# Threshold search by a clamp between two prepared candidates, instead of a compare and an XOR

## What is computed

```python
probs = jax.nn.softmax(logits, axis=-1)
_, idx = jax.lax.top_k(logits.T, top_k)          # top_k = capacity = 8192 / 16 = 512
xe = xn[idx]
h = jax.nn.gelu(jnp.einsum('ecd,efd->ecf', xe, fc1_weight) + fc1_bias[:, None, :], approximate=False)
y = jnp.einsum('ecf,edf->ecd', h, fc2_weight) + fc2_bias[:, None, :]
```

## Time and profile before

| | |
|---|---|
| Median of 3 runs | 980.95 us |
| The profiled execution | 983.5 us, its span 981.8 us |
| Granted TensorE clock, mean | 0.929 of full |
| TensorE matmul busy | 861.1 us (88%) |
| VectorE busy | 747.0 us (76%) |
| ScalarE busy | 505.8 us (52%) |
| GpSimd busy | 591.7 us (60%) |

### The profile page before, as it was taken

One profiled execution on the slowest core, in us unless ns is written; L12 is line 12 of the kernel. 1 busy time (PEld: TensorE's weight loads), 2 busy tenths in 40 slices (PEclk: granted clock), 3 DMA queues, 4 the chain that ended last, 5 costly groups with the idle time before them and its releaser, 6 DMA issues. The chain is left out here.

```text
span 981.8 us, 20963 instructions
## 1 busy us (share of the span) xinstructions
PE 861.1 (88%) x6115; PEld 737.1 (75%) x6115; DVE 747.0 (76%) x1660; ACT 505.8 (52%) x921; POOL 591.7 (60%) x564
## 2 busy tenths in 40 slices
PE   7899999999999999998711149999999999999995
PEld 6678887888788887886510037989999999999985
DVE  4488888888888888887388965898777777777642
ACT  1356556655566556655256206465555555555531
POOL 4256667666676667665442264688876776775344
PEclk8799999999999999999755559999999999999998
DMA  5266666666566656654232033366766555665333
GB/s 161 92 202 226 207 207 206 213 219 208 192 212 222 207 204 205 212 193 157 75 103 83 3 88 127 113 196 181 183 162 157 159 155 161 161 175 153 85 70 43
DMA packets 129540, 156.51 MB, mean 159 GB/s; under 512 B 22464, under 2 KB 104656, under 8 KB 129376
## 3 DMA queue, kind: packets, MB, share of 16 engines
q1 hardware_dynamic: 104096, 113.06, 35.5%
q0 software_dynamic: 15616, 25.70, 12.1%
q10 hardware_dynamic: 9792, 17.31, 4.8%
HBM read 74.93 MB, written 26.28 MB: 103 GB/s over the span
## 5 line engine op out<-in xcount | busy, mean ns | idle before, releaser
L587 DVE TENSOR_REDUCE NM<-bank 128x4 f32<-128x480 f32 x256 | 155.4, 649 | 59.9 <-PE bank L745 59.9
L418 ACT ACTIVATE PT<-bank 120x512 f32<-120x512 f32 x256 | 142.8, 603 | 35.9 <-PE bank L770 34.7
L349 POOL TENSOR_SCALAR XN<-X,mv,rstd 128x256 f32<-128x256 f32 x124 | 150.5, 1222 | 14.1 <-POOL rstd L344 13.3
L1658 PE MATMUL bank<-W2H,HH 128*128 128x256 f32 x512 | 145.5, 284 | 2.0 <-issue 2.0
L1660 PE MATMUL bank<-W2H,HL 128*128 128x256 f32 x512 | 144.3, 282 | 0.0
L1659 PE MATMUL bank<-W2L,HH 128*128 128x256 f32 x512 | 144.3, 282 | 0.0
L1119 POOL DMA_INDIRECT out_dram<-C,IO x60 | 109.6, 1827 | 52.2 <-issue 31.3
L1387 DVE TENSOR_TENSOR HL<-hf,HH 128x512 fp32r<-128x512 f32 x128 | 87.5, 691 | 49.8 <-ACT HH L1542 49.3
L545 DVE RECIPROCAL RR<-RC 128x256 f32<-128x256 f32 x64 | 111.6, 1743 | 8.6 <-DMA RC<-PVS 8.6
L770 PE MATMUL bank<-QX,KX 128*120 128x256 f32 x512 | 110.8, 309 | 8.2 <-DMA QX<-NMT 5.0
L1537 ACT ACTIVATE hf<-bank,B 128x512 f32<-128x512 f32 x128 | 87.8, 686 | 40.9 <-PE bank L1660 35.6
(11 more groups left out here) (194 smaller groups left out, 1906.6 us busy)
## 6 DMA issues: line engine op xcount, KB each, us to landing
QX<-QH ACTq DMA_DIRECT2D x64, 256.0 KB
W<-w1T_dram SPq DMA_DIRECT2D x16, 1024.0 KB, 5.3
W<-w2T_dram SPq DMA_DIRECT2D x16, 1024.0 KB, 5.9
X<-x_dram SPq DMA_DIRECT2D x32, 256.0 KB, 3.0
QX<-QL SPq DMA_DIRECT2D x32, 256.0 KB
XB<-x_dram SPq DMA_DIRECT2D x32, 256.0 KB, 2.8
RC<-PVS SPq DMA_DIRECT2D x64, 128.0 KB, 2.1
OC<-PVS SPq DMA_DIRECT2D x64, 128.0 KB, 2.2
```

Of the source, the lines that this page charges most:

```text
L349: ins = pool.tensor_scalar(dst[:, t, :], src[:, t, :], mv[:, t, 0:1], rstd[:, t:t + 1], ALU.subtract, ALU.mult)
L418: act.activation(PT[u][0:M, HE * k:HE * (k + 1), :], score_bank(b, k // 2)[k % 2][0:M, :], ACT.Exp, scale=SCALE) \
L587: dve.tensor_reduce(NM[u][:, t, :].rearrange("p (f n e) -> p n e f", n=HN, e=HE)[:, n, :, :], smax_bank[q % 2][:, 0:4 * M].rearrange("p (e ...
L1658: pe.matmul(o, wh, xh, start=first, stop=False)
```

## The change

The total is now the signed distance to the limit, scaled by 2^113, so it is either below every candidate or above every candidate. The two candidates that can follow are prepared while the total is on its way, and one operation clamps the total between them: `min(max(total, nexts[0]), nexts[1])` gives `nexts[0]` for a negative total and `nexts[1]` for a positive one.

- The limit comes in by a third matmul, `same_big` times a column of the new tile `limits`, which stands first in each round's group and ahead of the wait for the count. The weights `same_big` are `same_e` times 2^113 in bf16; the columns stay fp16.
- The group's bank alternates between two (`sum_bank`).
- `nexts` is one XOR of the candidate with two masks, one column each (`steps`): the next bit, and the tried bit with the next bit. It stands ahead of the shift, which now moves both masks, and the wait between them falls away.
- `missed` and the XOR behind it become the one clamp, with the total as its tensor and the two columns of `nexts` as pointers. A round has two increments of `step_dve` instead of three.
- GpSimd's constants: the cast becomes a multiplication with 2^113, and a memset, a wait, four memsets and a wait are added.

```diff
-def search_constants(pool, consts, same_e, same_e_below, same_e16, zero_row):
+def search_constants(pool, consts, same_e, same_e_below, same_big, zero_row, limits):
...
-    pool.tensor_copy(same_e16[:, :], same_e[:, :]).then_inc(consts, 1)
+    pool.tensor_scalar(same_big[:, :], same_e[:, :], BIG, 0.0, ALU.mult, ALU.add).then_inc(consts, 1)
+    pool.memset(limits[:, :], 0.0).then_inc(consts, 1)
+    pool.wait_ge(consts, n + 3)
+    for v, limit in enumerate((GMAX, SMAX)):
+        whole = -math.copysign(math.floor(abs(limit)), limit)
+        pool.memset(limits[0:E, v:v + 1], whole).then_inc(consts, 1)
+        pool.memset(limits[2 * E:3 * E, v:v + 1], -limit - whole).then_inc(consts, 1)
+    pool.wait_ge(consts, n + 7)
...
-    minus_half_e = sb("minus_half_e", [P, P], FP16)
+    minus_half_e = sb("minus_half_e", [P, P], BF16)
...
+    sum_bank = bank[2:4]
...
-            m = 3 * ROUNDS * turn + (BASE + 3 * r)
+            m = 2 * ROUNDS * turn + (BASE + 2 * r)
...
-            dve.tensor_scalar(bit[(r + 1) % 2][:, :], bit[r % 2][:, :], 1, None, ALU.logical_shift_right) \
+            dve.wait_ge(bit_ready, ROUNDS * turn + (r + 2))
+            dve.tensor_scalar(nexts[:, :], steps[r % 2][:, :], cand[:, :], None, ALU.bitwise_xor).then_inc(step_dve, 1)
+            dve.tensor_scalar(steps[(r + 1) % 2][:, :], steps[r % 2][:, :], 1, None, ALU.logical_shift_right) \
                 .then_inc(bit_ready, 1)
-            dve.wait_ge(bit_ready, ROUNDS * turn + (r + 2))
-            dve.tensor_scalar(both[:, :], cand[:, :], bit[(r + 1) % 2][:, :], None, ALU.bitwise_xor).then_inc(step_dve, 1)
+            dve.wait_ge(step_dve, m + 1)
             dve.wait_ge(total_done, ROUNDS * turn + (r + 2))
-            dve.tensor_scalar(missed[:, :], cnt_bank[:, 0:1], GMAX if alone else SMAX, bit[r % 2][:, :], ALU.is_lt, ALU.mult) \
-                .then_inc(step_dve, 1)
+            dve.tensor_scalar(cand[:, :].bitcast(FP32), sum_bank[(r + 1) % 2][:, 0:1], nexts[:, 0:1].bitcast(FP32),
+                              nexts[:, 1:2].bitcast(FP32), ALU.max, ALU.min).then_inc(step_dve, 1)
             dve.wait_ge(step_dve, m + 2)
-            dve.tensor_scalar(cand[:, :], both[:, :], missed[:, :], None, ALU.bitwise_xor).then_inc(step_dve, 1)
-            dve.wait_ge(step_dve, m + 3)
...
-        dve.memset(bit[0][:, :], 1 << 30).then_inc(bit_ready, 1)
+        dve.memset(top_bit[:, :], 1 << 30).then_inc(bit_ready, 1)
+        dve.memset(steps[0][:, 0:1], 3 << 29)
+        dve.memset(steps[0][:, 1:2], 1 << 29).then_inc(bit_ready, 1)
...
+            own = sum_bank[r % 2][:, 0:1]
+            v = 0 if alone else 1
+            pe.matmul(own, same_big[:, :], limits[:, v:v + 1], start=True, stop=False)
             pe.wait_ge(count_ready, ROUNDS * turn + (r + 1))
-            ins = pe.matmul(cnt_bank[:, 0:1], same_e16[:, :], count16[:, :], start=True, stop=alone)
+            ins = pe.matmul(own, same_big[:, :], count16[:, :], start=False, stop=alone)
             if not alone:
                 pe.wait_ge(signs_ready, ROUNDS * turn + (r - ALONE))
-                ins = pe.matmul(cnt_bank[:, 0:1], minus_half_e[:, :], sign16[:, :], start=False, stop=True)
+                ins = pe.matmul(own, minus_half_e[:, :], sign16[:, :], start=False, stop=True)
             ins.then_inc(total_done, 1)
```

More of the change, by code:

```diff
@@ L3 @@
 from contextlib import ExitStack
+import math
 FP32 = mybir.dt.float32
@@ L47 @@
 SMAX = GMAX - NC * HT / 2
+BIG = 2.0 ** 113
 BASE = 3
@@ L937, in routed_phase @@
     LT, LP, odd, sign_of, _ = search_views(search_tiles)
-    same_e, same_e_below, same_e16, zero_row = search_consts
+    same_e, same_e_below, same_big, zero_row, limits = search_consts
     probs = sb("probs", [P, NT, E], FP32)
@@ L970, in routed_phase @@
     ranked2 = sb("ranked2", [P, 2, CT], FP32)
-    cand, missed, both = (sb(n, [P, 1], U32) for n in ("cand", "missed", "both"))
-    bit = [sb(f"bit{u}", [P, 1], U32) for u in range(2)]
+    cand, top_bit = sb("cand", [P, 1], U32), sb("top_bit", [P, 1], U32)
+    steps = [sb(f"steps{u}", [P, 2], U32) for u in range(2)]
+    nexts = sb("nexts", [P, 2], U32)
     missed_i, cand_i = (sb(n, [P, 1], I32) for n in ("missed_i", "cand_i"))
@@ L1121, in add_up @@
                     .then_inc(added, 16)
-        pool.tensor_scalar(minus_half_e[:, :], same_e16[:, :], -0.5, 0.0, ALU.mult, ALU.add).then_inc(weights_ready, 1)
+        pool.tensor_scalar(minus_half_e[:, :], same_big[:, :], -0.5, 0.0, ALU.mult, ALU.add).then_inc(weights_ready, 1)
         pool.iota(s_col[:, :], pattern=[[1, GT]], base=0, channel_multiplier=GT,
@@ L1216, in decide @@
                               accum_out=count16[:, :]).then_inc(count_ready, 1)
-            dve.tensor_scalar(bit[(r + 1) % 2][:, :], bit[r % 2][:, :], 1, None, ALU.logical_shift_right) \
+            dve.wait_ge(bit_ready, ROUNDS * turn + (r + 2))
+            dve.tensor_scalar(nexts[:, :], steps[r % 2][:, :], cand[:, :], None, ALU.bitwise_xor).then_inc(step_dve, 1)
+            dve.tensor_scalar(steps[(r + 1) % 2][:, :], steps[r % 2][:, :], 1, None, ALU.logical_shift_right) \
                 .then_inc(bit_ready, 1)
-            dve.wait_ge(bit_ready, ROUNDS * turn + (r + 2))
-            dve.tensor_scalar(both[:, :], cand[:, :], bit[(r + 1) % 2][:, :], None, ALU.bitwise_xor).then_inc(step_dve, 1)
+            dve.wait_ge(step_dve, m + 1)
             dve.wait_ge(total_done, ROUNDS * turn + (r + 2))
-            dve.tensor_scalar(missed[:, :], cnt_bank[:, 0:1], GMAX if alone else SMAX, bit[r % 2][:, :], ALU.is_lt, ALU.mult) \
-                .then_inc(step_dve, 1)
+            dve.tensor_scalar(cand[:, :].bitcast(FP32), sum_bank[(r + 1) % 2][:, 0:1], nexts[:, 0:1].bitcast(FP32),
+                              nexts[:, 1:2].bitcast(FP32), ALU.max, ALU.min).then_inc(step_dve, 1)
             dve.wait_ge(step_dve, m + 2)
-            dve.tensor_scalar(cand[:, :], both[:, :], missed[:, :], None, ALU.bitwise_xor).then_inc(step_dve, 1)
-            dve.wait_ge(step_dve, m + 3)
         dve.tensor_scalar(junk, LT, 0.0, None, ALU.is_ge, ALU.add, accum_out=count16[:, :]).then_inc(count_ready, 1)
-        dve.memset(bit[0][:, :], 1 << 30).then_inc(bit_ready, 1)
+        dve.memset(top_bit[:, :], 1 << 30).then_inc(bit_ready, 1)
+        dve.memset(steps[0][:, 0:1], 3 << 29)
+        dve.memset(steps[0][:, 1:2], 1 << 29).then_inc(bit_ready, 1)
         dve.wait_ge(total_done, 1)
-        then(dve.tensor_scalar(missed_i[:, :], cnt_bank[:, 0:1], GMAX, None, ALU.is_lt))
+        then(dve.tensor_scalar(missed_i[:, :], sum_bank[0][:, 0:1], 0.0, None, ALU.is_lt))
         then(dve.tensor_scalar(cand_i[:, :], missed_i[:, :], 31, 31, ALU.logical_shift_left, ALU.arith_shift_right))
         dve.wait_ge(bit_ready, 1)
-        then(dve.tensor_scalar(cand[:, :], cand_i[:, :].bitcast(U32), bit[0][:, :], None, ALU.bitwise_xor))
+        then(dve.tensor_scalar(cand[:, :], cand_i[:, :].bitcast(U32), top_bit[:, :], None, ALU.bitwise_xor))
         assert n[0] == BASE
@@ L1241, in _ @@
         decide(0, 30, True)
-        n[0] = BASE + 3 * 31
+        n[0] = BASE + 2 * 31
         dve.wait_ge(sum_ready, 4)
@@ L1557, in signs @@
         def signs(r):
-            act.wait_ge(step_dve, BASE + 3 * r)
+            act.wait_ge(step_dve, BASE + 2 * r)
             with nc.allow_low_precision(reason="a whole number of at most 512"):
@@ L1768, in program @@
         search_consts = [ctx.enter_context(nc.sbuf_tensor(name, shape, dt)) for name, shape, dt in
-                         (("same_e", [P, P], FP32), ("same_e_below", [P, P], FP32), ("same_e16", [P, P], FP16),
-                          ("zero_row", [P, CT], FP32))]
+                         (("same_e", [P, P], FP32), ("same_e_below", [P, P], FP32), ("same_big", [P, P], BF16),
+                          ("zero_row", [P, CT], FP32), ("limits", [P, 2], FP16))]
         search_tiles = [ctx.enter_context(nc.sbuf_tensor(name, shape, FP32)) for name, shape in
```

## The result

The changed kernel takes 986.0 us (median of 22 runs) against 983.71 for the kernel before on the same chip (22 runs): ratio 1.0037, 95% interval 1.0024 to 1.005. I had forecast 975.3 and a gain of 5.7 us; by the ratio it is 3.6 us slower (2.3 by the two medians), inside the half per cent that I called "same", outside my range and on the other side of no change.

A forecast was written before the change was run, and what follows sets the result against it. The prediction took VectorE's serial chain to bound the search and TensorE the expert loop. The clamp's -6.2 us and GpSimd's constants' +0.5 summed to -5.7, taking the median 980.95 to 975.3; range 972.5 to 979.8.

The forecast's parts named there:

- The round's path: Search rounds: one clamp replaces `missed` and the XOR, saving 0.20 us a round, 6.2 us over 31 rounds.
- a free pointer: Rival for the clamp: its second pointer costs nothing, saving 8.0 us less 0.5, giving 973.5; chance 0.15.
- a merged operation as dear as what it replaces: Rival for the clamp: only 0.06 us a round saved, gain 1.9 us less 0.5, giving 979.6; chance 0.08.
- The start of the clamp: Search rounds: the clamp starts 0.03 us behind the last matmul's end, in a round of 1.40 us.
- The masks: Search rounds: `nexts` and the shift finish by the time the total arrives, at no cost.
- the step doesn't leave the path: Search rival: `nexts` and the shift release the clamp 0.15 us late, losing 4.7 of 6.2 us, giving 980.0; chance 0.08.
- GpSimd's constants: Tail of attention: the added memsets and waits delay `ve` and are paid in full, 0.5 us, bounds 0.2 and 1.0.
- ScalarE: Search rounds with a weight copy: no cost, 0.07 us idle left; as rival bound 976.5, chance 0.10.
- the extra matmul: Search rounds: the limit's matmul, 0.19 us, fits in TensorE's 1.35 us idle time and costs nothing.
- the mixed types: Rival for the search's matmuls: bf16 with fp16 adds 0.39 us each, 23 us in all, giving 998; chance 0.04.
- The clock: Rival behind the search: full clock returns later, 10 us more products at the lower level cost 5, giving 980.3; chance 0.05.

The follow-up runs named there:

- e4_wait_before_shift: Changed kernel with the wait for `nexts` moved from between shift and clamp to between `nexts` and shift; ratio 1.004 to the kernel before.
- e1_single_columns: Changed kernel with `nexts` and the mask shift each made one column at a time, four operations instead of two; ratio 0.998 to the kernel before.
- e5_masks_in_psum: Changed kernel with the two-column masks `steps` in PSUM and the wait for `nexts` ahead of the shift; 976.66 us, ratio 0.9924 to the kernel before.
- e8_constants_three_times: Kernel before with the change's memsets and waits for the limits added three times over; ratio 1.0026 to the kernel before.
- e2: Kernel before with its mask tile `bit` two columns wide, all readers taking the first column; ratio 1.0064 to the kernel before.
- e7: Changed kernel with masks and `nexts` three columns wide instead of two, the third unused; ratio 1.0042 to the kernel before.
- e6_limits_at_start: As e5_masks_in_psum, with the memsets of `limits` and their waits moved to the kernel's start; 975.89 us, ratio 0.9928 to the kernel before.

## Why the prediction was wrong

**The round's path: right in mechanism, and the size of the clamp too.** The clamp was to take 0.278 and takes 0.276 to 0.280. So the second pointer costs the 0.06 read from the earlier trace rows, no run shows one that comes for nothing, and the rivals of a free pointer and of a merged operation as dear as what it replaces fall. With the latter falls the 61 ns, an estimate from the table in the Trainium skill ("VectorE: DVE Perf Modes", section "The TRN2 errata"), for the operation that went.

```profile
L1234 DVE TENSOR_SCALAR cand<-bank,nexts x31: 276/278/280, 497.2 to 552.7; 128x1 f32<-128x1 f32 x31
```

**The start of the clamp: a mis-sized term.** I let it start 0.03 behind the matmul, as `missed` does. It starts 0.10 behind (516.09, 516.19), because the change also leaves two waits in a row ahead of it (e4_wait_before_shift). I had counted the wait for `nexts` as free since `nexts` is early. The round is 1.48, not 1.40, and the saving 3.8 us (e1_single_columns against before), not 6.2. Moved, it is 5.7 (e5_masks_in_psum).

**The masks: the step that failed.** I wrote "I cost them at nothing", and named as their cover the accumulator read and the matmuls. The cost isn't in the operation's place or length but in what it shares. e1_single_columns and the changed kernel differ by it alone: 50.85 against 59.59, so 8.7 us. The rival "the step doesn't leave the path" came nearest, with a wrong cause and half the size: in the five rounds the clamp is indeed released by the masks. I had looked only at what VectorE's queue holds, not at what runs on GpSimd in those rounds, where before the change this subtraction starts in the round of the earlier trace rows:

```profile
517.29 4.52 POOL L1138 TENSOR_TENSOR W2L<-W,W2H 128x2048 fp32r<-128x2048 f32 x1 [3.67 <-ACT W2H L1578]
```

And the trace of before most likely has the effect already, in a line next to one that I used as the price of two pointers:

```profile
L524 DVE TENSOR_SCALAR XN<-X,mv,rstd x2: 395/1545/2695, 6.7 to 9.3; 128x256 f32<-128x256 f32 x2
```

```profile
5.84 1.79 POOL L362 MEMSET QX<- 128x2048 f32 x1
6.73 3.01 DVE L524 TENSOR_SCALAR XN<-X,mv,rstd 128x256 f32<-128x256 f32 x2
7.58 1.69 POOL L363 MEMSET KX<- 128x1920 f32 x1
```

It is the same operation in the same shape as that of the earlier trace rows, at 2.695 us instead of 0.408. It starts during the first of two GpSimd memsets that write SBUF one behind the other, and it ends at 9.43, 0.16 behind the second. A line whose longest instruction is seven times its shortest should have been asked for its neighbours.

The Trainium skill names the mechanism. Its page "SBUF — State Buffer", section "Who interferes with whom", says that VectorE and GpSimd share a pair of ports, that whichever issues first keeps it for its whole instruction, and that copy, cast and tensor_scalar can take it while the form that also writes its accumulator can't. The Trainium skill, "VectorE: DVE Perf Modes", section "Mode 2×_2P", gives the condition: source and destination in SBUF, and an outermost dimension, not counting those of length one, that is even, or odd and equal on both sides. The runs agree with what they can show of both pages, which are the times and not the ports: held at two and at three columns (3.78), not at one (0.210), not from PSUM (0.216), and the counts, which write an accumulator, keep their 0.745 beside the same GpSimd work. By this rule, and with the 4.5 us of a subtraction in the trace of before, the change's forecast would have been a saving less four or five blocks of up to 4.5 us, and the likeliest case would have been slower. One thing in the trace of before isn't explained by the order of issue: `XN` had been waiting since 6.73 and was still held by the memset that began at 7.58.

**GpSimd's constants: right in mechanism, too small.** 0.5 was forecast, `ve` starts 1.16 behind the last table's start instead of 0.38, so 0.8. The term that was too small is the start of one memset behind the other: those of `limits` start 0.15 apart and not 0.04.

```profile
463.82 0.30 POOL L909 TENSOR_SCALAR same_big<-same_e 128x128 bf16<-128x128 f32 x1
464.07 0.09 POOL L910 MEMSET limits<- 128x2 f16 x1
464.22 0.09 POOL L914 MEMSET limits<- 16x1 f16 x1
464.37 0.09 POOL L915 MEMSET limits<- 16x1 f16 x1
...
464.98 0.19 POOL L344 TENSOR_SCALAR ve<-mv 128x2 f32<-128x2 f32 x1 [0.22 <-POOL limits L915]
```

Why 0.15 isn't shown. It isn't the 16 partitions alone: at the start of the kernel before, `no_max` is set on 16 partitions too and starts 0.03 behind the memset ahead of it (1.52, 1.55). That it is paid in full holds (e8_constants_three_times).

**ScalarE, the extra matmul, the mixed types: right.** ScalarE starts within 0.01 us of VectorE in the rounds of 1.41 with a copy too (e4_wait_before_shift, 516.00). The limit's matmul runs behind the total, 0.17 long, and the count's keeps 0.19 at the most. The price of the rival with the mixed types was misread, though: the earlier trace rows has two matmuls in its 0.58, and one takes 0.36, so the rival stood for 10 us and not 23.

```profile
L1644 PE MATMUL bank<-counts,same_e x2: 353/362/372, 552.4 to 552.7; 128*128 128x2 f32 x2
```

The count's and the limit's in the changed kernel:

```profile
L1645 PE MATMUL bank<-count,same_big x32: 183/187/187, 494.7 to 552.4; 128*128 128x1 f16 x32
L1643 PE MATMUL bank<-limits,same_big x32: 163/165/186, 493.7 to 550.5; 128*128 128x1 f16 x32
```

**The clock: a rival of the right kind with the gain, not the loss.** The rest of the span differs, as far as I can follow it, by the clock and, before the search, by the 0.8 us of constants. The granted clock is 0.91 up to 20 us and 0.87 from there to 60 in the changed kernel, against 0.83 in both stretches before, and the last table's operation starts 0.92 earlier (463.82, 464.74). The first fence is of before, the second of the changed kernel: stretch, then busy us of PE, PEld, DVE, ACT and POOL, then the granted clock.

```profile
480.00:486.00 6.00, 4.96 (x20) 4.02 (x20) 1.44 (x3) 0.33 (x1) 1.84 (x2) 0.72 0.12 44
602.70:607.20 4.50, 4.50 (x13) 3.54 (x14) 2.03 (x5) 0.69 (x1) 2.17 (x3) 0.62 0.27 87
```

```profile
480.00:486.00 6.00, 4.15 (x28) 3.70 (x28) 1.77 (x6) 0.84 (x2) 2.97 (x4) 1.00 0.25 87
606.40:611.00 4.60, 4.60 (x20) 3.83 (x21) 2.32 (x6) 2.08 (x4) 2.31 (x2) 1.00 0.28 86
```

The second expert's first products begin at 602.69 and at 606.40. Before, the clock falls back to its lower level within them (0.62 on average), after the change it doesn't (1.00). It is the same in the projection of the tail at 480.67 and 480.92, 3.68 us long before and 1.99 after; in the 6 us from 470 on it is the other way round, 0.72 before and 0.50 after. In the profiles, what follows the reciprocal takes 432.3 us before the change, 432.1 in e1_single_columns and e5_masks_in_psum, 430.5 after the change, and 429.1 to 429.3 in e2, e7 and e8. So the five whose search ended later than that of before (552.97 to 558.09 us) got 1.7 to 3.3 us back in these profiles, which goes with the ratios of the slow kernels being milder than their searches. It isn't a rule: e6_limits_at_start, which ends its search earliest (543.87), has 430.3, and the gain of e5_masks_in_psum is above its own search too (7.5 us, 4.9 to 9.9, where search less constants give 4.9). Nor is what comes before the search steady from one profile to the next: the first count starts between 493.3 and 495.0 in eight of the ten, but at 499.48 in e5_masks_in_psum and at 499.97 in e8_constants_three_times, where the granted clock from 20 to 60 us is 0.74 and 0.79 instead of 0.83 to 0.91. So the whole is judged here by the runs' times and a profile only by its search. What ties the clock's level to the moment of the search's end wasn't tried, and stays open.

## What to carry to other kernels

Before an operation is made two columns wide to save one, look at what the engine beside it does in the same microseconds: the duration of an operation is that of its queue only while it shares nothing. A line's minimum, median and maximum should be read together, for a maximum far above the rest in the trace of before is a price that the change may make common. When a change reorders semaphore waits, leave one wait, and the one that comes last, directly ahead of the operation on the path.

## What the runs showed of the hardware

- A VectorE XOR or shift on two elements a partition, SBUF to SBUF, waits for the end of a GpSimd subtraction that has begun: 3.78 us instead of 0.22. One column (0.210 at most), or the source in PSUM (0.216), avoids it; three columns don't (3.78).
- Each pointer operand of a one-column VectorE operation costs 0.06 us: 0.16 with none, 0.218 with one, 0.278 with two, all from PSUM.
- A wait on VectorE that is satisfied already, here for 0.17 us, costs 0.07 us if it stands directly ahead of the wait that releases an operation.
- GpSimd's memsets of one column on 16 partitions, all in the tile `limits`, start 0.15 us apart; small memsets of different tiles start 0.03 to 0.04 apart. What makes the difference isn't shown.
